# Layer 0: the order in which GpSimd adds a tile's two convolution products

## What is computed

```python
hs  = group_norm(x)                              # 32 groups
xs  = hs @ in_proj_w.T                           # 768 -> 1536 channels
xs  = depthwise_conv3x3(xs) + conv_b             # nine taps a channel
u   = xs * sigmoid(xs)
dt, Bs, Cs = split(u @ x_proj_w.T)
delta = softplus(dt @ dt_w.T + dt_b)
state_t = exp(delta*A) * state_(t-1) + delta*u*Bs   # four states, along 4096 tokens
y   = sum_n(state_n * Cs_n) + D*u
out = layer_norm(y) @ out_proj_w.T
x   = x + out
```

## Time and profile before

| | us |
|---|---|
| three runs: median (lowest, highest) | 3446.38 (3440.83, 3447.3) |
| the profiled execution's own time | 3447.7 |
| its span in the trace | 3445.2 |
| PE busy / DVE / ACT / POOL | 3331.1 / 2839.9 / 2413.8 / 2347.8 |
| line 1220, 180 instructions | 244.2 busy, 125.8 idle before |
| line 1223, 180 instructions | 229.6 busy, 27.3 idle before |

### The profile page before, as it was taken

The page is one execution under the profiler, slowest core; times in us unless marked ns, Lnnn a source line. Parts: engine busy times, 40 slices in busy tenths (PEclk is TensorE's granted clock), DMA queues, the critical chain, the costliest instruction groups (busy, mean ns, idle before and its releaser), DMA issues. The chain is left out here.

```text
span 3445.2 us, 38993 instructions
## 1 busy us (share of the span) xinstructions
PE 3331.1 (97%) x10712; PEld 1703.5 (49%) x10712; DVE 2839.9 (82%) x4072; ACT 2413.8 (70%) x4194; POOL 2347.8 (68%) x1561
## 2 busy tenths in 40 slices
PE   5999999999999999999999999998999999999999
PEld 2433443434434343443434344343358877777887
DVE  7889999999999999999999999998763355565532
ACT  3777888888888888888888888887655565433211
POOL 3587999999999999999999999989830011022210
PEclk9999999999999999999999999999999999999999
DMA  9544555565655656555565555555632233366654
GB/s 384 176 102 110 144 153 152 143 169 138 158 145 150 163 137 170 145 155 139 151 165 150 153 147 153 140 148 158 172 106 67 65 103 106 123 217 213 211 193 162
DMA packets 213688, 528.31 MB, mean 153 GB/s; under 512 B 25096, under 2 KB 46280, under 8 KB 208352
## 3 DMA queue, kind: packets, MB, share of 16 engines
q1 hardware_dynamic: 170944, 376.39, 33.3%
q0 software_dynamic: 42528, 149.45, 20.7%
HBM read 344.60 MB, written 80.48 MB: 123 GB/s over the span
## 5 line engine op out<-in xcount | busy, mean ns | idle before, releaser
L656 PE MATMUL p_in<-both_u,win_v 128*128 128x512 f32 (+1 forms) x2208 | 999.7, 600 | 30.2 <-ACT halo L1003 22.7
L683 PE MATMUL p_op<-both_u,rings_f 128*128 128x512 f32 x2016 | 905.6, 599 | 9.8 <-DVE rings_f L1332 9.8
L1248 POOL TENSOR_TENSOR rings_e<-rings_e,rings_f 128x2048 f32<-128x2048 f32 x191 | 866.4, 4536 | 18.8 <-DMA rings_f<-bc_scratch 4.0
L1292 DVE TENSOR_TENSOR_SCAN p_da<-p_da,state,rings_e 128x512 f32<-128x512 f32 x672 | 827.4, 1277 | 43.8 <-issue 26.7
L1317 DVE SCALAR_TENSOR_TENSOR p_cv<-win_v,conv_w,p_cv 128x512 f32<-128x512 f32 x924 | 695.7, 753 | 34.7 <-ACT p_cv L943 14.6
L656 PEld LDWEIGHTS p_in<-both_u,win_v 128*128 128x128 f32 x2208 | 411.7, 192 | 588.1 <-issue 584.7
L683 PEld LDWEIGHTS p_op<-both_u,rings_f 128*128 128x128 f32 x2016 | 375.5, 190 | 527.1 <-issue 508.2
L924 ACT ACTIVATE p_da<-rings_e,A 128x512 f32<-128x512 f32 x768 | 499.4, 682 | 12.6 <-ACT state L929 0.2
L1298 DVE TENSOR_TENSOR rings_e<-p_da,rings_f 128x512 f32<-128x512 f32 x768 | 487.4, 676 | 0.0
L1820 PE MATMUL banks<-x_split,w_split 128*128 128x512 f32 x1152 | 457.4, 397 | 6.8 <-PEq L471 4.2
L1822 PE MATMUL banks<-x_split,w_split 128*128 128x512 f32 x1152 | 449.9, 391 | 0.0
(11 more groups left out here) (289 smaller groups left out, 4148.7 us busy)
## 6 DMA issues: line engine op xcount, KB each, us to landing
rings_e<-rings_e POOLq DMA_DIRECT2D x192, 512.0 KB, 5.3
win_v<-in_win SPq DMA_DIRECT2D x192, 384.0 KB, 3.1
rings_f<-wout_scratch SPq DMA_DIRECT2D x180, 384.0 KB, 4.4
x_ring<-x_scratch SPq DMA_DIRECT2D x186, 256.0 KB, 2.7
q_scratch<-q_ring POOLq DMA_DIRECT2D x96, 256.0 KB, 2.6
x_split<-q_scratch SPq DMA_DIRECT2D x96, 256.0 KB, 3.4
out<-x_ring POOLq DMA_DIRECT2D x90, 256.0 KB, 2.9
rings_f<-in_x SPq DMA_DIRECT2D x84, 256.0 KB, 4.7
```

The source lines that it names most:

```text
L656: last = nc.tensor.matmul(bank_in(i)[:, 0:n], WR[:, i % NW, t, :], XN[:, t, off:off + n], start=(t == 0), stop=(t == XT - 1))
L683: last = nc.tensor.matmul(p_op[:], OR[:, e % NO, k - h * HALF, :], ucol(c * K + k), start=(k == 0), stop=(k == K - 1))
L1248: nc.gpsimd.tensor_tensor(G[:, i % NG], DU[:].unsqueeze(1).broadcast_to([P, NS, N]), BB[:], ALU.mult).then_inc(s_dbu, 1)
L1292: nc.vector.tensor_tensor_scan(bank, bank, G[:, i % NG, n, :], init, ALU.mult, ALU.add)\
```

## The change

`additions(b)` now waits for both products, adds the first buffer into the second, and only then waits for DVE's last tap and adds that sum to u. There are two additions as before, of the same size and with the same semaphore counts. The first one no longer touches u.

```diff
                 def additions(b):
-                    pool.wait_ge(s_ct, summed(b) + 1)
+                    pool.wait_ge(s_ct, summed(b) + 2)
+                    nc.gpsimd.tensor_tensor(CT[:, 1], CT[:, 1], CT[:, 0], ALU.add).then_inc(s_conv, 1)
                     pool.wait_ge(s_tap, len(TAPS) * (b + 1))
-                    nc.gpsimd.tensor_tensor(ucol(b), ucol(b), CT[:, 0], ALU.add).then_inc(s_conv, 1)
-                    pool.wait_ge(s_ct, summed(b) + 2)
                     pool.wait_ge(s_conv, summed(b) + 1)
                     nc.gpsimd.tensor_tensor(ucol(b), ucol(b), CT[:, 1], ALU.add).then_inc(s_conv, 1)
```

## The result

The changed kernel took 3439.74 us (median of 21 runs, 3436.30 to 3442.91). The kernel before, run beside it, took 3444.99 (21 runs, 3440.83 to 3450.85). The ratio is 0.9985, with a 95% interval of 0.9979 to 0.9991: faster by 5.25 us. That is less than the 6.9 us that I had named as the least that can be told from no change; with 21 runs of each, the interval still lies clear of 1. Predicted were 3442.2 us, within 3433 to 3449, and a gain of 5.5 against the one profiled execution (4.2 against the median of that time).

What follows compares the result with a forecast made beforehand. DVE (294.6 of 300 us busy) and PE (296.0) were taken to bound the kernel, not POOL. Steady part 4.2 plus ramp 1.3 made 5.5 us off the profiled 3447.7, so 3442.2, range 3433 to 3449.

Steps and rivals of the forecast that it cites:

- POOL's spare time is not the kernel's: Steady part: POOL's 121.3 us of waits for DVE's last tap are its own spare time; POOL itself counted at 0.
- POOL's slot, 4.47 to 3.56 us: DMA issue to input product: up to 0.9 us gained in waiting slots, the excess spent waiting for DVE at the DMA issue.
- ACT's 0.36 at the x_dbl sums: Once a chunk, two products each come about 0.18 us sooner, moving line 969 and the waiting PE up some 0.36.
- DVE's waits: Waits for ACT's decays, 300 to 2400 us: 15.9 falling to about 11, each gaining the smaller of itself and 0.36.
- The sum of the steady part: Steady part: 2.8 us from pair slots plus 1.4 from four other waits, 4.2 in all; bounds 0 and 15.9.
- The 0.58 at 2246.88: Share of DVE's 2.55 us wait there counted as gain, since two products ahead were late by 0.48 and 0.10.
- The ramp, 1.9 - 0.6 = 1.3: Before the first scan: PE's restart gains 1.9 us, a product waiting for the inner sum loses 0.6; bounds -0.6 and 1.9.
- The end, layer 1: Past the last tile's addition nothing waits for line 1223, and layer 1 is untouched: 0.
- Waits that only move: Rival: each wait is replaced by the next, nothing gained in the steady part; 3446.4 us, chance 0.20.
- All waits go: Rival: earlier products free all 15.9 us of DVE's waits and 1.9 in the ramp; 3429.9 us, chance 0.12 including any gain over 9.
- Contention: Rival: inner sum slows DVE's last tap, about 0.5 us in 115 slots, +58 to 3506; chance 0.07 including unseen causes.
- The change not doing what it says: Rival: POOL comes so late that nothing lies under the tap in any slot; 3447.7 us, chance 0.03.

Runs made afterwards that it cites:

- e4: Kernel before, with the new order only for the ten of twelve tiles from 28 to 191 with b mod 12 = 1 to 10; 3443.14 us, ratio 0.9997.
- e5: Changed kernel with both additions cut to 64 of 512 columns, the rest of the products left out; 3440.10 us, ratio 0.9988.
- e3: Kernel before, with the new order only for tiles 28 to 191 with b mod 12 = 11 or 0; 3441.61 us, ratio 0.9990.
- b_copy2: The kernel before run once more, unchanged; 3443.22 us in one run, against 3444.25 beside it.
- the copies: Repeat executions of the kernel before and of the changed kernel, nothing altered; 3443.22 and 3442.95 us for the former, 3441.78 for the latter.
- c2: Changed kernel with only tiles 179 and 180, ahead of the last x_dbl sums, in the old order; 3438.34 us, repeated at 3438.65.
- the five executions: The five executions with the new order in the whole ramp and full-size additions; `centre` of tile 14 started at 166.01 to 167.41 us.

## Why the prediction held, step by step

- **POOL's spare time is not the kernel's.** Held. POOL's waits for the tap fell by 79.3 us from 300 to 2400 us, and the kernel gained 2.8 between tiles 40 and 180. e4 shows it most plainly, and e5 shows that more of the same buys nothing.
- **POOL's slot, 4.47 to 3.56 us, with the rest turning up at the DMA issue.** Held to the hundredth in the slot shown. The inner sum shows as 1.55 us in the mean, where the second add is 1.27, since it now nearly always begins while the issue of 0.88 is still shown (719.02 against 718.41 + 0.88); it costs nothing.
- **ACT's 0.36 at the x_dbl sums, and PE at once after it.** Held: 0.39, and PE's waits of 6.7 us are 2.4. e3 shows that these are the tiles that count.
- **DVE's waits.** Predicted about 11 us left of 15.9; measured 10.9. That this fits is partly luck: 2.55 of the 5.0 us that went are the wait at 2246.88, of which the sum had counted 0.58, and b_copy2, in the old order, has 14.0 and not 15.9. The seven waits of about 0.20 in pair slots went, as predicted. The rule "the smaller of its wait and 0.36" failed at others: 0.77 at 1048 us, 0.42 at 1148 and 0.34 at 1597 (counted as 1.06 together) are 0.77, 0.43 and 0.35 in the changed kernel. Against that, the 1.65 at 1447 fell to 1.19, and a silu wait of 0.51 at 1234 to 0.32, where 0.36 and nothing had been counted. The other waits behind the silu stay where they were, most at 0.37.
- **The sum of the steady part.** Between tiles 40 and 180 the steps gave 3.1 (the pair slots there and two of the four others); 2.76 was measured (1746.22 - 1743.46), and by the copies 2.35 to 2.79. The 0.58 at 2246.88 I had priced as the order's doing. By the order of its own two tiles it was nothing: c2, with that place in the old order, takes 61.22 to tile 185, the changed kernel 61.21. In its place stands the clock: 1.1 to 1.3 us in the copies (62.34, 62.55 against 61.21), 2.65 in the one profile that I predicted from. That step failed, as a cause more than as a size: DVE's 2.55 us wait there, read as two late products, lay behind matmuls at half the clock.
- **The ramp, 1.9 - 0.6 = 1.3.** Both halves exist; the first profile shows 1.3, the five executions 0.3 to 1.7, in the mean 0.9. The mechanism held, down to "PE is then in its own order". I took the wait of one execution as if every execution had it.
- **The end, layer 1.** 0 in both. The first pair of profiles differs there by 2 us more (8.1 to 10.2), but so do two executions of one kernel: from the start of the last tile to the end the changed kernel took 1084.6 us in one and 1087.7 in the other, the kernel before 1084.5 to 1086.7.
- **The sum.** 0.9 for the ramp, 2.8 between tiles 40 and 180 and 1.2 for the clock, if that is the change's, make 4.9, against 5.25 in the medians. (Between tiles 29 and 40 the first pair shows 0.41 more, but executions of the kernel before differ by 0.9 there.) That it meets the predicted 5.5 is in part luck: 1.2 us came by a road that I had not seen, and about as much that I had counted did not come.
- **The rivals.** Waits that only move: refuted, by the 2.8 us between tiles 40 and 180 and by a ratio whose interval ends at 0.9991. All waits go: refuted, for 10.9 us of them are left; e5 adds that they are not POOL's. Contention: refuted. The last tap lies at 747 to 750 ns, although in 151 of the 152 cases an inner sum of POOL runs beside it. That fits the rule weighed in the prediction (the Trainium skill, "SBUF — State Buffer", section "SBUF: two separate sides"), by which a VectorE operation locks the shared ports only in a 2-port mode or with two inputs in SBUF; the tap has one of its inputs in PSUM. The change not doing what it says: refuted by line 933's waits.

## What to carry to other kernels

A GpSimd or ScalarE with spare time can still be on the path, through one short link once a loop: find the place where the bounding engines wait, follow it back to the few instructions that feed it, and change only those; here 2 tiles of 12 carried the whole steady gain, though ten others held most of the visible waiting. A gain of a few microseconds is read from the starts of the same instruction in both traces, not from totals. And look at a wait of the first profile in a second profile of the same kernel before putting a price on it.

## What the runs showed of the hardware

- PE entered the ramp up to 1.8 us later in one execution than in another of the same program (127.85 and 129.65 us), and a lead gained beside it was worth 1.7 or 0.3 us accordingly.
- PE's granted clock fell for some microseconds behind waits of 1.70 and of 2.49 us, and did not fall behind others of 1.70 and of 2.48 to 2.49. It cost 0.5 to 2.7 us each time. The length of the wait alone does not decide it: the clock fell in four of seven executions with the longer wait and in one of seven with the shorter (1.69 to 1.89 us).
- DVE's tap, with one input in SBUF and one in PSUM, lasted 747 to 750 ns with an addition of POOL beside it in 151 of 152 cases, and 748 to 749 in the kernel before, where 59 of 152 had one.
